# A transformer layer on one core: the row maxima of attention 56 units ahead, in couples beside the projections, with the fold of a pair put behind the next pair's first unit

## What is computed

```python
xn = layernorm(x)
Q, K, V = xn @ Wq + bq, xn @ Wk + bk, xn @ Wv + bv        # 16 heads of 16
scores = einsum('bqhd,bkhd->bhqk', Q, K) * scale + alibi
attn   = softmax(scores) @ V ; a = attn @ Wo + bo
router = xn @ Wg ; top 2 of 8 experts, softmax of the two logits
y = sum over experts of w * (silu(xn@W1) * (xn@W2)) @ W3 + (silu(xn@Ws1) * (xn@Ws2)) @ Ws3
out = x + a + y
```

## Time and profile before

| | before |
|---|---|
| median of 3 runs | 2412.12 us (2408.34 to 2413.84) |
| the profiled execution | 2409.6 us, of it 2407.8 us span |
| TensorE matmul busy | 2372.0 us, 99% |
| VectorE busy | 2003.8 us, 83% |
| ScalarE busy | 1715.7 us, 71% |
| GpSimd busy | 1062.4 us, 44% |
| TensorE matmuls | 19962 |

### The profile page before, as it was taken

How to read it: one execution, slowest core, us unless ns; L and a number is a source line. 1 busy time by engine, 2 the same in 40 slices (tenths; PEclk the granted TensorE clock), 3 DMA queues, 4 the chain that set the end, 5 groups by cost and what they waited for, 6 DMA issues and landing times.

```text
span 2407.8 us, 51776 instructions
## 1 busy us (share of the span) xinstructions
PE 2372.0 (99%) x19962; PEld 1574.0 (65%) x19962; DVE 2003.8 (83%) x3124; ACT 1715.7 (71%) x3279; POOL 1062.4 (44%) x1029
## 2 busy tenths in 40 slices
PE   7999999999999999999999999999999999999998
PEld 5775444444444444444444446999999988988898
DVE  7887999999999999999999983777777775555555
ACT  3444888888889888888888897777777763233332
POOL 3332455654324555445455333433443354445444
PEclk9997999999999999999999999999999999999999
DMA  8995454543323434444344333777777764334442
GB/s 283 341 315 179 138 171 140 173 151 109 90 80 106 133 114 134 120 115 127 107 125 119 109 107 115 241 245 237 236 240 246 237 192 126 106 105 128 131 110 88
DMA packets 219958, 383.28 MB, mean 159 GB/s; under 512 B 53908, under 2 KB 141076, under 8 KB 210596
## 3 DMA queue, kind: packets, MB, share of 16 engines
q1 hardware_dynamic: 181744, 219.30, 30.0%
q0 software_dynamic: 36880, 159.87, 20.8%
q10 hardware_dynamic: 1088, 0.79, 0.1%
HBM read 247.99 MB, written 140.31 MB: 161 GB/s over the span
## 4 chain that ended last, share of the span: by engine, by line
PE 91%; DVE 6%; issue 1%; ACT 1%; DMA 1%; POOL 0%; SPq 0%; DVEq 0%; ACTq 0%; POOLq 0%
PE ps L511 89%; PE ps L524 2%; DVE mx L965 2%; DVE mx L968 2%; DVE xn L939 0%; DVE stats L904 0%; DMA xr<-Xn 0%; SPq L1474 0%; DMA xt<-in_x 0%; POOL rstd L1173 0%; DVE qkL L955 0%; DMA OPS<-Alid 0%; DVE XL L947 0%; ACT qkH L794 0%; DVE WB0c L1067 0%
## 5 line engine op out<-in xcount | busy, mean ns | idle before, releaser
L965 DVE TENSOR_REDUCE mx<-ps 128x1 f32<-128x512 f32 x1316 | 826.1, 681 | 19.1 <-PE ps L511 19.0
L511 PE MATMUL ps<-OPS 54*128 54x512 f32 (+1 forms) x4096 | 787.6, 451 | 2.0 <-DMA OPS<-Alid 0.3
L511 PEld LDWEIGHTS ps<-OPS 54*128 54x128 f32 (+1 forms) x4096 | 373.1, 186 | 462.9 <-ACT pta L809 201.0
L809 ACT ACTIVATE pta<-ps 128x512 f32<-128x512 f32 x1024 | 541.0, 598 | 80.9 <-PE ps L511 67.9
L809 ACT ACTIVATE ptb<-ps 128x512 f32<-128x512 f32 x1024 | 538.5, 599 | 74.5 <-PE ps L511 73.6
L968 DVE TENSOR_REDUCE mx<-ps 128x2 f32<-128x1024 f32 x366 | 445.7, 1218 | 9.3 <-PE ps L511 2.5
L511 PE MATMUL ps<-OPS,WB 128*128 128x256 f32 (+2 forms) x2364 | 384.4, 315 | 3.1 <-DVE VB L1084 1.5
L511 PEld LDWEIGHTS ps<-OPS,WB 128*128 128x128 f32 (+1 forms) x2364 | 332.2, 182 | 28.2 <-issue 3.9
L511 PE MATMUL ps<-pta,VB 128*32 128x352 f32 (+1 forms) x4096 | 304.1, 392 | 0.1
L511 PE MATMUL ps<-ptb,VB 128*32 128x352 f32 (+1 forms) x4096 | 302.1, 390 | 0.0
L1222 POOL TENSOR_SCALAR m<-m 128x16 f32<-128x16 f32 x64 | 18.3, 286 | 475.8 <-DVE m L972 475.8
(11 more groups left out here) (169 smaller groups left out, 2925.0 us busy)
## 6 DMA issues: line engine op xcount, KB each, us to landing
OPS<-QKh SPq DMA_DIRECT2D x512, 64.0 KB
Xs<-zero POOLq DMA_DIRECT2D x71, 256.0 KB, 3.1
xr<-Xs SPq DMA_DIRECT2D x71, 256.0 KB
Ys<-VB SPq DMA_DIRECT2D x71, 256.0 KB
QKh<-qkH SPq DMA_DIRECT2D x16, 1024.0 KB, 7.0
QKl<-qkL SPq DMA_DIRECT2D x16, 1024.0 KB, 8.8
OPS<-QKl SPq DMA_DIRECT2D x256, 64.0 KB
asum<-Sd SPq DMA_DIRECT2D x64, 256.0 KB
```

The lines of the kernel that those rows point to most:

```text
L511: return self.e.matmul(o, l, r, start=start, stop=stop)
L809: self.e.activation(pt(m)[:, half * GT:(half + 1) * GT], ps[:, n % 3, :], ACT.Exp).then_inc(sem["exp"], 1)
L965: self.e.reduce_max(mx[:, r % 2, hh, i, half:half + 1], ps[:, bank, :], AX.X).then_inc(sem["mxred"], 1)
```

## The change

Beside the projections the units run in couples, two after each of the listed places: (1, 5) for groups 5 to 12, (1, 3, 5, 7) for group 13, six places in group 14 and (1, 3) in group 15, which makes 56. They rotate over banks 2, 3 and 7; for that the transposes of all groups use banks 0 and 1. A new function `unit` numbers the units: for pairs 0 and 1 the two units of a couple are of different heads (different halves of the array's rows), from pair 2 on the numbering is as before. `ORDER0` goes, all pairs use `ORDER`, and the maxima stay 56 units ahead. The last three V projections of group 15 move into the first double-step (L in `FIRST_STEP`), in bank 3. `DOUBLE` has four entries, and doubles are used from pair 2 on instead of pair 3. The fold of a pair is issued behind the first unit of the next one. `max_rows(r+1)` is issued in the third double-step of pair r (kc = 4, before), where it was in the first; `place_rows(r+1)` in the fourth (kc = 6), where it was among the loads after the first. `finish_v(15)` and `begin_heads` come after the first double-step.

```diff
-AHEAD = 64
-UNITS = (0, 2, 5, 7)
+UNITS = (1, 5), (1, 3, 5, 7), (1, 2, 3, 5, 6, 7), (1, 3)
+MAX_BANKS = (2, 3, 7)
 ORDER = "SuSuSuPSuSuSuPSuSuP"
-ORDER0 = "SuuSuuSuuPSuSuuSuPSuuSuP"
-DOUBLE = (2, 4, 6, 10, 12, 14)
+FIRST_STEP = "SuSuSuLSuSuLSuSuLSu"
+DOUBLE = (2, 6, 10, 14)
...
-            for o in range(8):
+            for o in range(8 if g < NG - 1 else 5):
...
-                if g >= FIRST and o in UNITS and n < AHEAD:
-                    self.max_unit(n, 7)
-                    n += 1
-            self.finish_v(g)
+                if g >= FIRST and o in UNITS[max(g - NG + 4, 0)]:
+                    for i in range(2):
+                        self.max_unit(n, MAX_BANKS[n % 3])
+                        n += 1
+            if g < NG - 1:
+                self.finish_v(g)
...
-        self.begin_heads()
...
-            i = v = 0
-            for c in ORDER if r else ORDER0:
-                if c == "S":
+            i = v = last = 0
+            for c in FIRST_STEP if s == 0 else ORDER:
+                if c == "L":
+                    last += 1
+                    self.project_v(NG - 1, last)
+                elif c == "S":
...
-                    if v == 1 and kc == (0 if r else 4) and r + 1 < NPAIR:
+                    if v == 0 and kc == 4 and r + 1 < NPAIR:
                         self.max_rows(r + 1)
...
+            if s == 0:
+                self.finish_v(NG - 1)
+                self.begin_heads()
             if kc == 0:
                 self.next_pair(r)
-            elif kc == 6 and r == 0:
-                self.place_rows(1)
-            elif kc >= 4 and r >= 1:
+            elif kc == 6 and r + 1 < NPAIR:
+                self.place_rows(r + 1)
+            if kc >= 4 and r >= 1:
                 self.heads(r - 1, kc // 2 - 1)
...
-            if i == 1 and 1 <= r and r + 1 < NPAIR:
-                self.place_rows(r + 1)
...
+def unit(n):
+
+    r, u = divmod(n, 32)
+    if r < 2:
+        return r, 1 - u % 2, u // 4, u // 2 % 2
+    return r, 1 - u // 2 % 2, u // 4, u % 2
...
             def max_unit(self, n, bank=None):
...
-                    self.w.wait_ge("mxred", n)
+                    self.w.wait_ge("mxred", n - 2)
...
+                if n == 2:
+                    self.w.wait_ge("mxred", ring.turns[0][1])
...
-                if u // 2 not in DOUBLE or r < 3:
+                if u // 2 not in DOUBLE or r < 2:
...
-                if u == 31:
-                    self.w.wait_ge("mxred", n + 1)
-                    self.w.wait_ge("mnl", r - 1)
-                    self.e.tensor_reduce(m16[:, r % 2, :, :], mx[:, r % 2, :, :, :], AX.X, ALU.max).then_inc(sem["m16"], 1)
+                if u == 0 and r:
+                    self.fold(r - 1)
+                elif n == 32 * NPAIR - 1:
+                    self.fold(r)
+
+            def fold(self, r):
+
+                self.w.wait_ge("mxred", 32 * (r + 1))
+                self.w.wait_ge("mnl", r - 1)
+                self.e.tensor_reduce(m16[:, r % 2, :, :], mx[:, r % 2, :, :, :], AX.X, ALU.max).then_inc(sem["m16"], 1)
```

More of the change, by code:

```diff
@@ L410, in build @@
         Wvst = sbuf(A, "Wvst", [P, 2, D + NE])
-        Wv = {k: sbuf(A, "Wv" + k, [P, 2, D + NE], F32R) for k in ("h", "l")}
         bqk = sbuf(A, "bqk", [P, 4])
-        bvr = sbuf(A, "bvr", [P, D])
         nhalf = sbuf(A, "nhalf", [P, 4])
@@ L423, in build @@
         vs = sbuf(A, "vs", [P, 2, 4, D + NE])
+        Wv = {k: sbuf(A, "Wv" + k, [P, 2, D + NE], F32R) for k in ("h", "l")}
+        bvr = sbuf(A, "bvr", [P, D])
         Wost = vs[:, 1, 0:2, 0:D]
@@ L527, in columns @@
                 w = self.w
-                b = 2 * (g % 2)
                 w.wait_ge("c_ident", 16)
                 w.wait_ge("norm", 2 * g + 2)
-                w.wait_ge("xh", g - 1)
-                w.wait_ge("xl", g - 1)
+                w.wait_ge("xh", g)
+                w.wait_ge("xl", g)
                 for c in range(2):
                     for j in range(4):
-                        last = self.turn(ps[:, b + c, j * P:(j + 1) * P], xn[:, g % 3, j, c * P:(c + 1) * P])
+                        last = self.turn(ps[:, c, j * P:(j + 1) * P], xn[:, g % 3, j, c * P:(c + 1) * P])
                 last.then_inc(sem["xt"], 1)
@@ L558, in project_v @@
                 k = g % 2
-                bank = self.project_bank(8 * g + 4 + j)
+                if g < NG - 1 or j == 0:
+                    bank = self.project_bank(8 * g + 4 + j)
+                else:
+                    bank = 3
+                    self.w.wait_ge("mxred", ring.turns[0][1])
+                    self.w.wait_ge("vev", 4 * g + j)
                 self.mm3(ps[:, bank, 0:D + NE], [(XH[:, k, c, j * P:(j + 1) * P], XL[:, k, c, j * P:(j + 1) * P],
@@ L573, in ring_bank @@
                 else:
-                    self.w.wait_ge("vev", 4 * NG)
+                    self.w.wait_ge("qkh", 4 * NG)
+                    self.w.wait_ge("qkl", 4 * NG)
+                    self.w.wait_ge("vev", 4 * (NG - 1) + 1)
                     if at == 3:
@@ L579, in max_unit @@
             def max_unit(self, n, bank=None):
-                r, u = divmod(n, 32)
-                hh, i, half = 1 - u // 2 % 2, u // 4, u % 2
+                r, hh, i, half = unit(n)
                 k, h0 = r % 4, 64 * hh
@@ L614, in values @@
                         self.w.wait_ge("acc1", r)
-                        self.w.wait_ge("xh", NG)
-                        self.w.wait_ge("xl", NG)
+                        self.w.wait_ge("vev", 4 * NG)
                     for hh in range(2):
@@ L781, in columns @@
             def columns(self, g):
-                b = 2 * (g % 2)
                 self.w.wait_ge("vmm", 4 * (g - 1))
                 self.w.wait_ge("xt", g + 1)
-                self.e.copy(XH[:, g % 2, :, :], ps[:, b:b + 2, :]).then_inc(sem["xh"], 1)
+                self.e.copy(XH[:, g % 2, :, :], ps[:, 0:2, :]).then_inc(sem["xh"], 1)
             def project_qk(self, g, o):
@@ L797, in project_v @@
             def project_v(self, g, j):
-                k, bank = g % 2, 4 + (8 * g + 4 + j) % 3
+                k, bank = g % 2, 4 + (8 * g + 4 + j) % 3 if g < NG - 1 or j == 0 else 3
                 self.w.wait_ge(f"vs{k}", 16 * (g // 2))
@@ L805, in scores @@
                 if m % NPT >= NPT // 2:
-                    projections_over(self.w)
+                    for k in range(2):
+                        self.w.wait_ge(f"qh{k}", 16 * NG // 2)
+                        self.w.wait_ge(f"ql{k}", 16 * NG // 2)
                 self.w.wait_ge("pv", m // 2 - 3)
@@ L959, in max_unit @@
             def max_unit(self, n, bank=None):
-                r, u = divmod(n, 32)
-                hh, i, half = 1 - u // 2 % 2, u // 4, u % 2
+                u = n % 32
+                r, hh, i, half = unit(n)
                 bank = ring.bank("max", n) if bank is None else bank
-                if u // 2 not in DOUBLE or r < 3:
+                if u // 2 not in DOUBLE or r < 2:
                     self.w.wait_ge("mxmm", n + 1)
```

4 lines of the change are left out of this document (2 added, 2 removed).

## The result

| | before | after |
|---|---|---|
| median of 20 runs each | 2409.81 us (2407.18 to 2416.13) | 2425.85 us (2415.33 to 2438.94) |
| ratio of the two | | 1.0062, 95% interval 1.0050 to 1.0073 |
| the profiled execution | 2409.6 us | 2436.05 us, of it 2434.2 us span |

I had forecast 2388 us and a range of 2371 to 2407. The kernel came out 16 us slower than before, outside the range. The last of my rivals (the rows of the maxima come late in every pair) is what happened, apart from its size at single pairs.

What follows compares the result with a forecast made beforehand. VectorE bounds attention, TensorE close below. Start 197.0 plus 1.4, pairs 1185.4, router 9.5, hand-over 7.3, idle 2, rows 4, clock 2 gave 1408.6 for 1432.9, 24.3 us less: 2385.3 profiled, median 2388, range 2371 to 2407.

Steps and rivals of the forecast that it cites:

- The last of my rivals: Attention pairs: SyncE's loads, write, read and landings form a loop, rows late every pair; x = 0.8, 2437 us; chance 0.12.
- Rows of the maxima: Attention: rows just in time, hidden by TensorE's bank lead except in seven even pairs up to 14; 4 us (0 to 10).
- Start of attention: End of projections: couples and three V projections sent away save 6.0 us, so attention starts at about 197.
- the couples' gain: Projection groups 5 to 12: two couples save 1.0 us a group, taken as 0.6 (0 to 1.0).
- My third rival: Projections: VectorE's 10.62 us becomes the bound, 5.1 us for groups 5 to 12 stay away; 2393 us; chance 0.05.
- The rule on PSUM that I had weighed: Projections: tiling speeds TensorE but not the emptying of PSUM by VectorE; by it the couples' gain is absent.
- The hand-over: Start of attention: VectorE stands 7.3 us (4 to 9) for GpSimd's chain and tables; one short clock fall, 2 us.
- The steady pair: Attention: VectorE's work takes 19.12 us a pair, 62 pairs 1185.4 us, against a pair of 19.3 before.
- the idle 0.22: VectorE's idle 0.22 us a pair before a double on a double-step's first two places; taken as gone, 2 us left over.
- The part for doubles: VectorE in attention: two doubles less cost 0.11 us a pair and remove the idle 0.22 us.
- the fold: VectorE in attention: the fold behind a unit of the next pair gives back its wait of 0.12 us.
- Experts unchanged: Stage of the experts after attention: no change in its time.

Runs made afterwards that it cites:

- the last experiment: Kernel with pair 3's key-side loads issued later: VectorE takes XL ahead of the next norm's first half instead of behind it; 2374.52 us, ratio 0.9842.

## Why the prediction was wrong, point by point

- *Rows of the maxima: 4 us taken (0 to 10), 46 to 50 measured.* The step that failed is a term's size and reach, not its mechanism. I worked out rows issued at 16.8 us of a pair for a need at 19.1, "on the edge", and then declared it hidden by TensorE's lead in the ring of banks. It is not hidden: rows issued at 17.1 (11.6 after the sum copy) or later delay the next pair one for one, because TensorE has no other work once it is at the next pair's scores. SyncE issued the store earlier than I said, at 13.9 on average for 14.9. But I took its landing as 1.9 us from the earlier trace rows, a pair whose 512 KB load had gone out 12 us before, and it was 3.41 on average, up to 4.6 beside a 512 KB load from pair 26 on and up to 5.5 in the first fifteen. I let the rows be late in seven pairs only, by the reciprocal, which the experiment with the rows ahead of the reciprocal shows to be innocent. The argument against the rival, that a late TensorE finds its banks empty and the fold then comes earlier, was wrong too: the store can't go out before SyncE's loads are through, and in no pair from 1 to 59 it goes out earlier than 7.77 us after the sum copy.
- *The clock in pairs: not foreseen.* In six pairs the clock fell behind a wait for the rows, and these hold 15.9 of the 22.2 us left over above.
- *The rival.* It asked for x = 0.8 us a pair and gave 2437 at 0.12. In the profiled execution x is 50 / 61 = 0.82 and the time 2436; the median of 2426 is 10 us less. The nearness is part luck: the rival had the landings at 2.5 us in every pair, where they were 2 in some and 5 in others, and no clock falls. The direction of the evidence was in my own text: a margin of 0 to 1.5 us, a landing from quiet rows. It deserved about even odds.
- *Start of attention: 197 forecast, 203.0 measured.* The projections gave 3.2 us of the 6.0, since the hold of the norm ate most of the couples' gain (0.3 us a group for 0.6; 0.84 once it was gone), and the wait for pair 0's rows, a transfer I had not followed, took 3.16 us. My third rival (couples buy nothing) named VectorE's work as the bound. It was a hold of the norm, not work. The rule on PSUM that I had weighed (the Trainium skill, TensorEngine Tiling (Array Packing), PSUM Bottleneck) pointed to the right engine; the last experiment shows that the emptying of PSUM was not the limit, as the groups fell to 10.92 us with VectorE emptying the same banks.
- *The hand-over: 7.3 forecast, 5.88 measured,* with two falls of the clock of 6.8 us where I had one short one. Right in its chain; the store landed faster (GpSimd waited 3.8 us for it, not 5.05).
- *The steady pair: 19.12 forecast, 19.00 measured on time.* Right, and the idle 0.22 did go. The part for doubles is confirmed by itself (0.10 of 0.11), of the fold only half (0.07 of 0.12).
- *Experts unchanged:* 939.5 us in the profiled execution of after and 933.5 in that of before, but 933 to 940 in the profiles of the other kernels, which don't differ there; it varies by execution.

From the forecast's 1408.6 to the measured 1452.5: rows +46, start +6, hand-over and clock +1, steady pair -7 (62 x 0.12), and -2 unexplained. The 6 us of the stage of the experts come on top, which makes 50 of the 51 us between 2385 and the profiled 2436.

## What to carry to other kernels

A result that travels between engines by small DMAs has a slack, and the slack must be compared with the landing under the traffic of that moment and with what stands ahead in the issuing queue, not with the landing in a quiet stretch; where the margin comes out as about zero, it is a cost in every turn of the loop. Bringing work "just in time" frees one resource once, but exposes its latency each time; take the gain (here the cheaper reductions) and leave the lead, or move bulk loads behind the small transfer and the small transfer forward: the fastest kernels here keep the 56. And when an engine looks full, look at how long its same instruction takes at two places before calling it the bound.

## What the runs showed of the hardware that I had not expected

- In pairs 26 to 58 a store of 16 KB lands in 1.95 to 2.8 us where no 512 KB load is in flight and in 3.0 to 4.6 us in all but two of those with one; moving the loads alone brought pair 30 back from 4.38 to 1.96. The Trainium skill (DMA: Bandwidth & Descriptors, Latency and other measured facts) gives 0.2 us on average and 2 us at high load for the access to HBM, by which a landing would grow by 1.8 us. From 1.95 it grows here by 1 to 2.7 us beside such a load, at its most by more than that; that the access to HBM is the cause, no run shows.
- VectorE's norm stands 2.50 us instead of 0.40 while GpSimd adds 128 x 1024 elements, and one exchange of two steps gave 6 us of the whole.
- Two unit matmuls on different halves of the array's rows stretch the stream by 0.64 us, on the same half by 0.87.
- A 1 MB store issued 4.2 us earlier landed only 1.7 us earlier, in a stretch (198.68 to 209.23) where the DMA share was 0.83.
